# Moving the last batch's query/key products and the residual sums, and leaving out repeated waits, in a kernel that feeds three engines tile by tile

## Time and profile before

| | |
|---|---|
| three executions | 2201.06, 2201.24, 2204.51 us |
| profiled execution, own time | 2205.13 us |
| its span, first to last instruction | 2203.8 us |
| TensorE busy | 1978.9 us (90%) |
| VectorE busy | 1916.8 us (87%) |
| ScalarE busy | 1831.1 us (83%) |
| GpSimd busy | 993.3 us (45%) |
| mean granted clock of TensorE | 0.974 of 2.4 GHz |

### The profile page before, as it was taken

One profiled execution on the slowest core, in us unless ns is written; L12 is line 12 of the kernel. 1 busy time (PEld: TensorE's weight loads), 2 busy tenths in 40 slices (PEclk: granted clock), 3 DMA queues, 4 the chain that ended last, 5 costly groups with the idle time before them and its releaser, 6 DMA issues.

```text
span 2203.8 us, 41207 instructions
## 1 busy us (share of the span) xinstructions
PE 1978.9 (90%) x16914; PEld 756.5 (34%) x16914; DVE 1916.8 (87%) x2852; ACT 1831.1 (83%) x1232; POOL 993.3 (45%) x478
## 2 busy tenths in 40 slices
PE   6889989988989999987899999879999999899967
PEld 3323233222223333221233233212332335677633
DVE  4699899898999999999999999999999997544328
ACT  3599999998999999999899999998999994122214
POOL 1110010010327648633457467234494583477747
PEclk9999999999999999999999999999999999899979
DMA  7416434525421203032212121321111207699888
GB/s 242 160 51 210 130 117 139 201 66 182 159 98 35 90 23 116 18 137 76 81 34 78 32 108 54 108 87 61 61 52 63 70 4 186 174 240 244 211 219 305
DMA packets 184576, 259.93 MB, mean 118 GB/s; under 512 B 22728, under 2 KB 162632, under 8 KB 176200
## 3 DMA queue, kind: packets, MB, share of 16 engines
q1 hardware_dynamic: 169904, 237.84, 32.6%
q0 software_dynamic: 12288, 18.88, 4.6%
q10 hardware_dynamic: 2200, 0.60, 0.1%
HBM read 187.25 MB, written 70.03 MB: 117 GB/s over the span
## 4 chain that ended last, share of the span: by engine, by line
DVE 26%; POOL 20%; PE 12%; issue 5%; DMA 3%; ACT 2%; SPq 0%; DVEq 0%; POOLq 0%; ACTq 0%
POOL scr L1751 13%; DVE TB L1574 12%; DVE TB L1592 6%; PE ps L864 2%; PE ps L1023 2%; DMA y_rows<-ZB 2%; POOL scr L1749 2%; PE ps L1115 2%; DVE ZB L1574 2%; PE ps L870 1%; ACT TB L1237 1%; PE ps L1138 1%; DVE st L1296 1%; POOL rs L1740 1%; PE ps L1084 1%
## 5 line engine op out<-in xcount | busy, mean ns | idle before, releaser
L1237 ACT ACTIVATE TB<-ZB,nzk 128x2048 f32<-128x2048 f32 x778 | 1491.0, 1998 | 77.6 <-DMA ZB<-zq_rows 42.7
L1023 PE MATMUL ps<-TB,V 128*32 128x512 f32 x7272 | 941.2, 607 | 114.7 <-DVE TB L1574 99.6
L1574 DVE TENSOR_SCALAR TB<-TB 128x2048 f32<-128x2048 f32 x778 | 923.9, 1218 | 17.2 <-ACT TB L1237 17.0
L1751 POOL TENSOR_TENSOR scr<-ebase,scr 128x256 f32<-128x256 f32 x12 | 515.0, 42913 | 0.0
L1023 PEld LDWEIGHTS ps<-TB,V 128*32 128x32 f32 x7272 | 202.7, 110 | 643.8 <-DVE TB L1574 344.2
L1592 DVE TENSOR_SCALAR TB<-ZB,held 128x2048 f32<-128x2048 f32 x261 | 341.7, 1342 | 0.0
L1721 POOL TENSOR_SCALAR ve<-mv 128x4 f32<-128x4 f32 x44 | 41.6, 944 | 402.3 <-DVE mv L1305 401.7
L1749 POOL TENSOR_TENSOR scr<-ebase,scr 128x4 f32<-128x4 f32 x12 | 55.7, 4644 | 363.0 <-DVE scr L1442 363.0
L1237 ACT ACTIVATE ZB<-ZB,nzk 128x2048 f32<-128x2048 f32 x102 | 203.9, 1999 | 6.2 <-PE ps L1023 6.2
L870 PE MATMUL ps<-XF,wsgu 128*32 128x512 f32 x1536 | 203.2, 601 | 6.2 <-DVE Sq L1325 6.2
L1269 ACT ACTIVATE ZB<-ps 128x128 f32<-128x128 f32 x64 | 17.7, 277 | 168.9 <-PE ps L1115 168.9
(11 more groups left out here) (211 smaller groups left out, 2085.2 us busy)
## 6 DMA issues: line engine op xcount, KB each, us to landing
ZB<-zq_rows SPq DMA_DIRECT2D x64, 1024.0 KB, 5.4
scr<-fused_w SPq DMA_DIRECT2D x32, 512.0 KB, 3.9
TB<-y_rows SPq DMA_DIRECT2D x24, 512.0 KB, 8.0
TB<-in_egu_w SPq DMA_DIRECT2D x44, 256.0 KB, 3.6
y_rows<-zero SPq DMA_DIRECT2D x20, 512.0 KB, 4.9
fused_w<-TB SPq DMA_DIRECT2D x4, 2048.0 KB, 14.2
scr<-fused_w SPq DMA_DIRECT2D x32, 256.0 KB, 2.7
XF<-in_x SPq DMA_DIRECT2D x24, 256.0 KB, 4.9
```

The lines of the kernel that those rows point to most:

```text
L1023: ins = pe.matmul(ps[k][32 * c:32 * c + 32, :], w, tile(e)[:, 512 * c:512 * c + 512], start=(first_of[q, j] == e), stop=(last_of[q, j] == e))
L1237: act.activation(tile(e), zrow(head), ACT.Abs, bias=nzk[b][:, kb * H + g:kb * H + g + 1], scale=1.0).then_inc(s_abs, 1)
L1574: dve.tensor_scalar(T, T, 1.0, 1.0, ALU.min, ALU.subtract).then_inc(s_bump, 1)
L1751: pool.tensor_tensor(E4[:, :, 0:64], view(ebase[:, 0:1], 0, [[0, 4], [0, 64]]), E4[:, :, 0:64], ALU.pow).then_inc(s_ex, 1)
```

## The change

The 32 pieces of the last batch's query/key products go from slots 1 + 3h//2 to 8 + 11h//8 (first piece at slot 8 and not 1, last at 50 and not 47), and their loads from 3h//2 - 4 to 11h//8. The residual sums go one slot later, r + 6 and r + 7, and their stores from r + 8 to r + 9. In quads 4, 8 and 12, the first of batches 1 to 3, the eight "c" letters stand at other places. A "c" clamp waits for the keys' columns only where it is the first of its quad, and for the query row only where it is the first of its head; a context write waits for the residual sums only once in a batch.

```diff
@@ PLACES, quads 4, 8 and 12
-    "acacacaaacaaaaaaacaaaacaaacaacaaaaaa",
+    "acaaaccaacaaacaaaaaacaaaaacaacaaaaaa",
-    "acaaacaaacaaaacaaacaaacaaacaacaaaaaa",
+    "acaaacaaacaaaacaaacaacaaaacaacaaaaaa",
-    "acaaacaaacaaaacaaacaaacaaacaacaaaaaa",
+    "acaaacaaacaaaacaaacaacaaaacaacaaaaaa",
@@ timetable(b)
-            sy += [(r - 4, "a", p, k), (r + 8, "x1", p, k)]
-            dv += [(r, "cst", p, k, 0), (r + 1, "cst", p, k, 1), (r + 2, "cst", p, k, 2), (r + 5, "cn", p, k, 0), (r + 6, "cn", p, k, 1)]
+            sy += [(r - 4, "a", p, k), (r + 9, "x1", p, k)]
+            dv += [(r, "cst", p, k, 0), (r + 1, "cst", p, k, 1), (r + 2, "cst", p, k, 2), (r + 6, "cn", p, k, 0), (r + 7, "cn", p, k, 1)]
...
     if b == 1:
         f = NB - 1
         for h in range(32):
-            pe += [(1 + 3 * h // 2, ("z", f), h)]
-            sy += [(3 * h // 2 - 4, "mh", f, h)]
+            pe += [(8 + 11 * h // 8, ("z", f), h)]
+            sy += [(11 * h // 8, "mh", f, h)]
@@ build: the first clamp of each quad and of each head
-        first_of, first_abs, last_of = {}, {}, {}
+        first_of, first_abs, first_clamp, last_of = {}, {}, {}, {}
...
+            if kind == "c":
+                first_clamp.setdefault(q, e)
+                first_clamp.setdefault((q, j), e)
@@ vector_quad_scale
-            if b:
+            if b and q % 4 == 0 and t == 0:
                 dve.wait_ge(s_xs, 4 * b)
@@ vector_clamp
-            if kind == "c":
+            if kind == "c" and first_clamp[q] == e:
                 dve.wait_ge(s_own, q + 1)
+            if kind == "c" and first_clamp[q, j] == e:
                 dve.wait_ge(q_zb[head % NZB], 16 * (head // NZB + 1))
```

## The result

The changed kernel takes 2190.18 us (median of 6 runs, 2183.95 to 2192.42), the kernel before 2201.15 us in the same comparison (6 runs, 2197.70 to 2204.51): a ratio of 0.9944 [0.993, 0.9958], 11.0 us less. The profiled execution took 2192.42 us, with a span of 2190.5.

The account below looks back on a forecast made before the run. ScalarE and VectorE were taken as full, so only their idle time can be won: products 6.3 + residual sums 4.1, letters and waits 0, make 10.4 us; 2201.2 - 10.4 = 2190.8 us, range 2183.5 to 2196.5.

Parts of the forecast that it names:

- The products: Start of batch 1: products eight slots later remove TensorE's wait for fused weights and the stops behind it; 6.3 us gained.
- The margins for pieces, residual loads and stores: Moved pieces and SyncE's later loads and stores still have slots to spare, so the move costs 0.
- The residual sums: Batches 1 to 3: one more tile before each sum partly covers VectorE's wait for GpSimd's factors; 4.1 us gained.
- k = 0 and k = 1 of batch 1: First two residual sums of batch 1: the added tile wins 0.6 of 1.38 us and 0.8 us.
- k = 2 of batches 2 and 3: Third residual sum there: the clamp pair moved to slot 37 lets GpSimd's power in early; 0.85 of 1.51 us won.
- The three stops that I had split between 0.75 and -0.1: Sums k = 2 of batch 1, k = 1 of batches 2 and 3: 0.75 if the power gets in, else -0.1.
- The letters: Clamped pairs moved by up to eight slots, hidden by ScalarE's ring of buffers: 0, bounds -3.9 and +3.9 us.
- The waits: Fewer semaphore waits at clamps and context writes: 0, since satisfied waits pass while a tile runs; upper bound 6.3 us.
- The tile covers the factors fully: Residual sums: GpSimd's chain ends when it did, so 6.3 + 11 = 17.3 us gained, 2183.9 us; chance 0.14.
- The stop only moves: Residual sums: GpSimd gets nothing between plain tiles, the stop moves behind the added tile; 7.7 us gained, 2193.5; chance 0.22.
- The start's stop was no loss: Start of batch 1: the stop cost nothing or returns at the eighth slot; 2197 to 2201 us; chance 0.09.
- The low clock in denser pieces: Batch 1, slots 8 to 24: TensorE at its low clock costs 25 us, 6.3 won back; 2220 us; chance 0.05.

Follow-up runs that it names:

- z_only: The kernel before with only the 32 products and their loads eight slots later: 2194.43 us, ratio 0.997.
- loads_first: The kernel before with the first three loads of fused weights issued ahead of eight loads of values: 2200.79 us, ratio 0.9995.
- pairs_in_chain: The changed kernel with one clamped pair moved two slots later in each of quads 4, 8 and 12: 2185.27 us, ratio 0.9926.
- waits_only: The kernel before with only the repeated waits left out: 2200.85 us, ratio 1.0.
- cn_only: The kernel before with only the residual sums and their stores one slot later, letters old: 2193.67 us, ratio 0.9967.
- old_letters: The changed kernel with the old order of letters in quads 4, 8 and 12: 2189.84 us, ratio 0.9948.
- best: The changed kernel with a clamped pair moved later, column sums copied four slots earlier, and factors before the product of means and factors: 2179.29 us, ratio 0.9889.
- factors_first: The changed kernel with GpSimd computing the factors before the product of means and factors: 2187.38 us, ratio 0.9924.
- column_sums_early: The changed kernel with VectorE's copy of the column sums at slot 78, not 82, of each batch: 2184.46 us, ratio 0.9924.
- no_factor_wait: The changed kernel with a constant column replacing GpSimd's factors in the residual sums, so these do not wait: 2185.58 us, ratio 0.9921.

## Why the prediction was right

It said 2190.8 us with 10.4 us gained; 2190.18 and 11.0 were measured. By its steps:

- **The products, 6.3 us.** Right in place and size: z_only took 6.46 us off quad 4 by this edit alone. VectorE's stops of 5.67 and 0.64 were the measure, not ScalarE's 7.32. That it came out to 0.2 us is in part luck: in the four traces with the old slots and the old order of loads the two stops come to 6.1, 6.3, 6.4 and 7.9 us, and the forecast had only the one of 6.3. The eight loads of values, which the prediction named with the stores as what held the first load, had no part in it (loads_first). The margins for pieces, residual loads and stores held: no matmul waited for `scr` at a later piece, and the residual sums wait for GpSimd alone. (The store of sums at slot 32 waits to slot 35, not 34, by the prediction's own rule; it had room.)
- **The residual sums, 4.1 us.** 1.7 in batch 1: quad 4 of the change is 1.59 shorter than that of z_only, right. 1.2 in each of batches 2 and 3: 0.97 and 0.96 came, one fifth less. Over single stops it was less exact. k = 0 and k = 1 of batch 1 won 0.72 and 0.85, where 0.6 and 0.8 were said; k = 2 of batches 2 and 3 won 0.85, as said. The three stops that I had split between 0.75 and -0.1 and booked at 0.3 all went the second way: they stayed at 1.51 with a power of 5.39 us, so GpSimd got nothing done among the three plain tiles. k = 0 of batches 2 and 3, booked at 0, won 0.13. And the sum of 9.9 us of stops is 0.9 above the 9 I gave for it.
- **The letters, 0.** Right to 0.5 us, and the 0.5 has a reason: in quad 4 the new letters put a clamped pair right behind the third sum's statistics, where the old ones have four plain tiles and, with the sum one slot later, a stop of 0.66. This is why 1.51 stayed there, and pairs_in_chain, which moved that pair two slots on, won 0.86.
- **The waits, 0.** Right: the stretch with tiles is 0.3 us longer in waits_only, where the bound was 6.3 less.
- **Their sum.** Quad 4 is 8.05 us shorter, where 8.0 was said. Without the 1.7 us of quads 9 and 10 the stretch with tiles is 9.9 us shorter, 0.5 less than the 10.4. Those 1.7 are TensorE's clock behind a stop that is in both kernels; I had named that stop as late next, but not that its price differs from one batch to another. In the profiled executions it hides the 0.5 that the residual sums fell short. The timed 11.0 against 10.4 is as near partly by luck, then: the prediction had no term for this clock, and the median of six runs that reach over 8 us could have come out some us to either side (the interval of the ratio is 9 to 15 us gained).

**The rivals.** *The tile covers the factors fully* needs stops near 2.5 us; 9.9 are left. *The stop only moves* would have left some 12 to 13 us of stops and won 1.4 us at most: it was right for the three stops at 1.51 and wrong for k = 1 of batch 1 (1.51 to 0.66). *The start's stop was no loss* fell with the 6.46 us of z_only. *The low clock in denser pieces* fell with the clock of 1.00 and a first piece of 1.04 us at slot 8. What was only argued before, that a tile in front covers the factors in part, is shown by cn_only (2.4 us less of stops in quad 4). That the place of a clamped pair among the tiles sets the stop is shown by old_letters and pairs_in_chain; that GpSimd needs a clamp to get in is not, since four plain tiles did as well. What decides whether GpSimd gets in between two plain tiles stays open: best and factors_first have the same order of tiles there and fell out differently.

## What to carry to other kernels

- When two engines are full, put what a stop costs at the idle time of the one that is the limit later in the stretch (6.3 us here, not 7.3), and move waiting work behind other work of the same engine: putting the load ahead of others gained at most 0.7 us of a 5.7 us stop, since the load itself waited for a store, and the move gained all of it.
- When VectorE waits for a few small GpSimd operations, first put the one it needs first (0.26 us each stop), then see what VectorE runs meanwhile: moving a clamped pair two slots away from the statistics took a power of 5.39 us down to 3.56, an added plain tile can lengthen GpSimd's operation by its own length (the median power went from 3.52 to 4.66 us).
- Compare stretch by stretch between equal points of the order. Here most repeat to 0.1 us while the ends of the program differ by 3 to 7, so that a term of 1 us can be told where the clock and the start's stop are not in it; and it shows a gain that was in no term of the forecast.

## What the runs showed of the hardware

- A TensorE stop of 2.06 us was followed by the 1.2 GHz level in some cases and not in others. By the granted clock, and by the quads' lengths in the table, it was in 20 of 30 (batches 1 to 3 of the ten kernels with the copy at slot 82): 6 of 10 in batch 1, 6 in batch 2, 8 in batch 3. A fall costs 1.5 to 1.7 us. In the nine cases without the stop the clock did not fall at this place; column_sums_early has a fall later in quad 13 (at 1556.8 us), behind another stop of 1.13 us.
- GpSimd's operations of 128 x 4 elements, 0.20 to 1.04 us where VectorE leaves room, took up to 5.4 us beside VectorE's back-to-back tiles, one plain scaling even 4.52 (best), and 12.46 us in no_factor_wait. The Trainium skill, "SBUF — State Buffer", section "Who interferes with whom", says that a VectorE instruction in a two-port mode and GpSimd share a pair of ports, and that whichever issues first has it for its whole instruction; that these operations end with a VectorE tile or 0.9 us behind one agrees with it. At 559 us GpSimd got in between two tiles in one kernel and not in the other, with the same order of tiles.
- Waits on semaphores that are long satisfied, 49 to 50 ns in their own records, cost nothing that shows beside tiles of 1.2 us: 125 of them fewer, ratio 1.0 [0.9987, 1.0014] (waits_only).
